# Last layer of a graph network kernel: the order of the second product's turn and copy, and how the maxima of the logits are taken

## What is computed

```python
a = (m1_s @ W_alpha).reshape(e, H, AS_)          # H = 4 heads
a = jnp.where(a > 0, a, 0.2 * a)
a = jnp.sum(a * alpha_dot, axis=-1, keepdims=True)
amax = jax.ops.segment_max(a, dst, num_segments=n)
ex = jnp.exp(a - amax[dst])
den = jax.ops.segment_sum(ex, dst, num_segments=n)
...
agg = jax.ops.segment_sum(alpha * h, dst, num_segments=n)
```

## Time and profile before

| | before |
|---|---|
| median of 3 runs | 12696.42 us (12687.43 to 12728.43) |
| the profiled execution | 12681.68 us, span 12679.8 us |
| PE busy | 8726.2 us (69%) |
| DVE busy | 7658.1 us (60%) |
| POOL busy | 7121.7 us (56%) |
| ACT busy | 4658.1 us (37%) |
| mean granted TensorE clock | 0.818 of full speed |

### The profile page before, as it was taken

The page is one execution under the profiler, slowest core; times in us unless marked ns, Lnnn a source line. Parts: engine busy times, 40 slices in busy tenths (PEclk is TensorE's granted clock), DMA queues, the critical chain, the costliest instruction groups (busy, mean ns, idle before and its releaser), DMA issues. The chain is left out here.

```text
span 12679.8 us, 243067 instructions
## 1 busy us (share of the span) xinstructions
PE 8726.2 (69%) x60118; PEld 6156.2 (49%) x60119; DVE 7658.1 (60%) x26426; ACT 4658.1 (37%) x15787; POOL 7121.7 (56%) x12018
## 2 busy tenths in 40 slices
PE   2222222278888567777757777868888888888887
PEld 1000000056666344444445555437777777777776
DVE  5333333356666443444434554878888888888887
ACT  0000000035555233333312221026666666666665
POOL 2666666645555344344336663017777777777775
PEclk8555555578888777777758888979999999999998
DMA  4000000022222211111123332930000000000000
GB/s 135 25 25 24 24 24 25 16 49 58 56 57 57 51 46 45 44 45 45 37 61 79 80 80 63 198 65 22 21 21 21 21 21 21 22 21 22 21 21 22
DMA packets 828472, 567.97 MB, mean 45 GB/s; under 512 B 588110, under 2 KB 763941, under 8 KB 825674
## 3 DMA queue, kind: packets, MB, share of 16 engines
q0 software_dynamic: 218720, 330.70, 9.8%
q1 hardware_dynamic: 596842, 196.50, 8.5%
q10 hardware_dynamic: 12480, 35.51, 0.8%
HBM read 482.70 MB, written 79.57 MB: 44 GB/s over the span
## 5 line engine op out<-in xcount | busy, mean ns | idle before, releaser
L585 PE MATMUL rank<-onehots,upper_h 128*128 128x427 f16 x812 | 407.5, 502 | 1683.9 <-remote 1014.9
L1327 POOL DMA_INDIRECT l1s_tile_rows<-node_table,l1s_tile_rows x864 | 835.3, 967 | 1260.1 <-DMA l1s_tile_rows<-rows_by_src 1018.7
L2444 POOL DMA_INDIRECT l_source_rows<-node_table,l_edge_rows x866 | 877.3, 1013 | 973.4 <-DMA l_edge_rows<-rows_by_dst 712.1
L908 POOL DMA_INDIRECT l_source_rows<-node_table,l_edge_rows x880 | 867.7, 986 | 743.4 <-DMA l_edge_rows<-rows_by_dst 393.1
L1710 POOL DMA_INDIRECT l2s_node_rows<-node_table,l2s_edge_rows x864 | 866.5, 1003 | 650.0 <-issue 243.0
L605 POOL DMA_INDIRECT rows_by_src<-row_s,pos_i x812 | 782.7, 964 | 706.7 <-issue 414.0
L585 PEld LDWEIGHTS rank<-onehots,upper_h 128*128 128x128 f16 x812 | 84.0, 103 | 2222.2 <-remote 1168.3
L605 POOL DMA_INDIRECT rows_by_dst<-row_d,pos_i x812 | 785.0, 967 | 270.6 <-issue 266.6
L1470 ACT COPY l1s_outer<-l1s_p_outer 128x1024 f32<-128x1024 f32 x304 | 307.4, 1011 | 1324.7 <-remote 885.3
L1740 PE MATMUL l2s_p_sum<-l2s_rows_by_edge,l2s_node_onehot 128*128 128x352 f32 x1728 | 695.0, 519 | 125.8 <-issue 125.3
L976 PE MATMUL l_p_sum<-l_messages,l_node_onehot 128*128 128x384 f32 x1728 | 676.0, 540 | 126.6 <-DVE l_messages L1025 81.0
(11 more groups left out here) (580 smaller groups left out, 27290.6 us busy)
## 6 DMA issues: line engine op xcount, KB each, us to landing
l_xv_by<-h_turned_l SPq DMA_DIRECT2D x120, 320.0 KB
l_source_rows<-node_table,l_edge_rows POOLq DMA_INDIRECT x1746
l_xs_by<-h_turned_l SPq DMA_DIRECT2D x40, 640.0 KB
rows_by_src<-pad_rows_s ACTq DMA_DIRECT2D x16, 1053.0 KB
l1s_tile_rows<-rows_by_src SPq DMA_DIRECT2D x216, 78.0 KB
l2s_edge_rows<-rows_by_src SPq DMA_DIRECT2D x216, 78.0 KB
l_edge_rows<-rows_by_dst SPq DMA_DIRECT2D x220, 72.0 KB
l_edge_rows<-rows_by_dst SPq DMA_DIRECT2D x433, 36.0 KB
```

The costliest lines, as they stand in the source:

```text
L908: pool.indirect_dma_start(xg[k][:, s, :], None, K["table0"], bass.IndirectOffsetOnAxis(ap=pay[k][:, s, D_SRC:D_SRC + 1].bitcast(U32), axis ...
L1327: pool.indirect_dma_start(ring[:, t, 0:XW], None, table, bass.IndirectOffsetOnAxis(ap=ring[:, t, XW + S_DST:XW + S_DST + 1].bitcast(U32), ...
L2444: pool.indirect_dma_start(xg[u][:, s, :], None, K["table0"], bass.IndirectOffsetOnAxis(ap=pay[u][:, s, D_SRC:D_SRC + 1].bitcast(U32), axis ...
```

## The change

On TensorE the six transpositions of the second product move ahead of the three front transpositions, and on ScalarE the copies of the turned second product move from behind the front copies to right behind tanh. `masked` becomes `spread_logits`: the product with `apart` is left out, and each head's product with `sel` starts its own sum. On ScalarE the bf16 copy of the one-hot is replaced by an affine copy to float32, 1e30 times (one-hot - 1), in four buffers named `apart`. On VectorE each reduction of 512 columns is replaced by `take_max`: a semaphore increment and, for each of the two heads, one fused instruction that adds the mask in SBUF to the logits in PSUM, writes the sum to SBUF and its maximum to a column of `qm`. `qm` moves from PSUM to SBUF, where L2732 reads it.

```diff
-        sel, apart = sb("sel", [P, HEADS, P], BF16), sb("apart", [P, P], BF16)
+        sel = sb("sel", [P, HEADS, P], BF16)
...
-            hot_t, hot_tb = four("onehot_turned", [P, PAIR * P]), four("onehot_turned_b", [P, PAIR * P], BF16)
-            pay_t = sbi("edge_rows_turned", [P, P])
+            hot_t, apart = four("onehot_turned", [P, PAIR * P]), four("apart", [P, PAIR * P])
+            pay_t, masked = sbi("edge_rows_turned", [P, P]), sbi("masked_logits", [P, 2, PAIR * P])
...
-            mn, drop, shrink = (sbi(n, [P, HEADS]) for n in ("new_max", "max_step", "shrink"))
+            qm, mn, drop, shrink = (sbi(n, [P, HEADS]) for n in ("pair_max", "new_max", "max_step", "shrink"))
...
-            qm = p_r[:, 0, 512 - HEADS:512]
...
-                    def masked(half, u):
-
-                        nc.tensor.matmul(p_m[:, :, :], apart[:, :], free(hot_tb[u][:, :], [0, 2], [1, PAIR * P]), start=True, stop=False, skip_group_check=True)
+                    def spread_logits(half):
+
                         for j in range(2):
-                            ins = nc.tensor.matmul(p_m[:, j, :], sel[:, 2 * half + j, :], a3_t[:, :], start=False, stop=True, skip_group_check=True)
+                            ins = nc.tensor.matmul(p_m[:, j, :], sel[:, 2 * half + j, :], a3_t[:, :], start=True, stop=True, skip_group_check=True)
...
-                            wait("a3_copied", -1)
-                            wait("rbf_scaled")
-                            wait("hot_made")
-                            front_turn(ahead_u)
-
                             for n in ("b_done", "b_scaled", "b_crossed"):
                                 wait(n, -1)
...
                                 ins.then_inc(m["g_turned"], 1)
+
+                            wait("a3_copied", -1)
+                            wait("rbf_scaled")
+                            wait("hot_made")
+                            front_turn(ahead_u)
...
-                    def front_halves(u):
-                        nc.scalar.copy(hot_tb[u][:, :], hot_t[u][:, :])
+                    def front_apart(u):
+                        nc.scalar.activation(apart[u][:, :], hot_t[u][:, :], ACT.Copy, bias=-NEVER, scale=NEVER)
...
                             nc.scalar.activation(th[:, :, :], logits[:, :, CS:D], ACT.Tanh, scale=0.5).then_inc(m["tanh_done"], 1)
+                            wait("heads_done", -1)
+                            for s in range(PAIR):
+                                wait("g_turned", 0, s + 1)
+                                nc.scalar.copy(g_t[s][:, :], p_t[:, s, 0:PT]).then_inc(m["g_copied"], 1)
                             wait("val_made", -1)
...
                             front((u + 1) % 4)
-                            wait("heads_done", -1)
-                            for s in range(PAIR):
-                                wait("g_turned", 0, s + 1)
-                                nc.scalar.copy(g_t[s][:, :], p_t[:, s, 0:PT]).then_inc(m["g_copied"], 1)
...
+                    def take_max(h, off):
+                        dve.sem_inc(m["dve_seen"], 1)
+                        for j in range(2):
+                            ins = nc.vector.tensor_tensor_reduce(masked[:, j, :], p_m[:, j, :], off[:, :], 1.0, -NEVER, ALU.add, ALU.max, qm[:, h + j:h + j + 1])
+                        ins.then_inc(m["max_taken"], 1)
...
-                            nc.vector.tensor_reduce(qm[:, 0:2], p_m[:, :, :], AX.X, ALU.max).then_inc(m["max_taken"], 1)
+                            take_max(0, apart[(u - 2) % 4])
...
-                            nc.vector.tensor_reduce(qm[:, 2:4], p_m[:, :, :], AX.X, ALU.max).then_inc(m["max_taken"], 1)
+                            take_max(2, apart[(u - 2) % 4])
...
-                            TT(mn[:, :], top_b, qm, ALU.max).then_inc(m["max_made"], 1)
+                            TT(mn[:, :], top_b, qm[:, :], ALU.max).then_inc(m["max_made"], 1)
```

11 lines of the change are left out of this document (5 added, 6 removed).

## The result

The changed kernel takes 12541.17 us (median of 6 runs, 12534.64 to 12582.6) against 12701.51 us for the kernel before, timed beside it (6 runs, 12687.43 to 12728.43). The ratio is 0.9877, 95% interval 0.9861 to 0.9892. It is faster by 1.2%, inside the range and on the forecast side, but by 160 us where 228 were forecast: the forecast's own range ended at 12540, so the time lies at its edge, towards the rival of growing blocks (12578). The profiled executions are 12681.68 and 12534.64 us, 147 us apart.

The account below looks back on a forecast made before the run. TensorE and VectorE were nearly full, TensorE waiting for ScalarE's copies; VectorE would become the bound. 3 x 0.47 + 0.70 = 2.11 us a pass, 108 passes, 228 us: 12468 us against the median; range 12335 to 12595.

Parts of the forecast that it names:

- the forecast's own range: Whole kernel: 12410 to 12540 us around 12468, VectorE the new bound with moderate blocks; chance 0.55.
- rival of growing blocks: "Blocks grow": L2732, L2734, L2736 and L2745 on VectorE each lose part of a GpSimd cross product; 12578 us, chance 0.20.
- a pair: Two fused 256-element sums on VectorE replacing one reduction: 0.68 us, 0.72 with 0.04 for the semaphore increment.
- The rival of half rate: Fused pair on VectorE runs at half rate, 0.53 us more per pair, twice a turn; 12926 us, chance 0.07.
- Nothing gained: Heads wait for the leaky step until S+6.16 as for the copies; only the pass start gains; 12690 us, chance 0.05.
- ScalarE's delays: Gate, dots' copy and front copies go about 0.5 to 0.9 us later in ScalarE's order; priced at nothing.
- the signs named: For blocks on VectorE: durations of L2732 and L2745 above their floor in many turns.
- the heads can start 0.37 after L2740 starts: TensorE's heads after VectorE's leaky step L2740: 0.27 for the step plus 0.1 for the signal.
- its 0.23 for blocks: Plain turn: 0.23 us added for VectorE operations blocked by GpSimd, between 0 - 0.15 and 0.5.
- the 1.04 taken: VectorE from L2730 to the leaky step L2740: 1.04 us in the turn shown, a small block already included.
- The pass start: Turn that starts each pass of four: heads earlier by 0.70 us, ends 0.5 and 0.8.
- the fused sums as 0.22 spent on VectorE: Each fused pair costs 0.11 us more than the reduction, 0.22 a turn, taking mask products off TensorE.

Follow-up runs that it names:

- the second increment: Changed kernel with `dve.sem_inc` written twice ahead of each pair of fused sums on VectorE; ratio 0.9885 to the kernel before.
- the leaky step last: TensorE's head products wait for the first copy, then the leaky step, tanh wait dropped: 0.9900 on the changed kernel, 0.9869 on the kernel with only the reordering.
- the copy in the gap: The last run: reordering alone, leaky step as TensorE's last wait, copy of the maxima moved between second product's dots and their sum; 10742.2 us, ratio 0.9844.
- the product put back: Changed kernel with one 512-column product, its result overwritten, ahead of each pair of head products; 12500.33 us beside 12624.41 before, single run.
- fewer waits: Kernel with only the reordering; TensorE waits for both copies at once, then the leaky step, tanh wait dropped; ratio 0.9858.
- two steps behind: Kernel with only the reordering; VectorE's sum of the dots and max step moved behind the leaky step and value sum; 12655.04 us, ratio 1.0015.
- e1: Kernel before with only the order of turns and copies changed, mask products and reductions kept; 12451.26 us beside 12624.41, ratio 0.9861.

## Why the prediction was right, and where it fell short

**Right: the mechanism.** The wait for ScalarE's copies turned into one on the leaky step; VectorE became full; L2516 is gone; the fused sums follow one another after 0.34 and a pair takes 0.69 (forecast 0.68, and 0.72 with its increment); VectorE's wait before the head spread is 0.13 (forecast under 0.2). The rival of half rate is refuted: 418 ns for 256 elements, which would have been near 685 (0.53 more a pair, half of it each). "Nothing gained" is refuted too: the heads start at S+5.89, not 6.16. ScalarE's delays cost nothing: no VectorE wait for the gate appears. "Blocks grow" is not what happened either: 0.46 for 0.36. But the blocks fell on other operations than the signs named. The new maximum is above its floor in 45% of the plain turns, the scaled leaky step in 8%; the max step and the copy of the maxima in 95% and more.

**The step that failed** is "the heads can start 0.37 after L2740 starts", with 0.1 for the signal. It measured 0.57: 0.27 for the leaky step, 0.15 for its signal, and 0.15 for the wait for the first copy, which stands behind it in TensorE's queue although its signal has long come. The plain turn, forecast with its 0.23 for blocks placed ahead of the leaky step, against the medians:

```
                 first max  L2733  leaky  heads  spread  turn
forecast         1.10       4.05   5.32   5.69   7.38    8.81
measured         1.25       4.16   5.32   5.89   7.58    9.01
```

The leaky step is where it was forecast by luck: two errors cancel, 0.11 late up to L2733 and 0.11 early from there. (a) The first maximum came 0.15 late: the head products do start 0.21 sooner, but the pair begins 0.19 after their end where the reduction began 0.04 after it; the second increment, at 0.10 each, puts most of the difference on the increment, priced at 0.04. (b) From L2733 to the leaky step it was 1.16, 0.12 more than the 1.04 taken, where 0.23 had been added. (The 1.04 of the turn shown in the earlier trace rows was a lightly blocked one; the median of the kernel before is 1.29. A piece of the chain that varies should be read over many turns.) From there on the whole miss is one term: 0.57 for 0.37. In 324 plain turns (three of each pass) this 0.20 is 65 us. The pass start, 9.51 against 10.09, gained 0.58 of its 0.70, within its ends, which in 108 passes is 13 us more. Together 78 us, where 68 are missing from the medians and 81 from the profiled executions (228 less 160, 228 less 147).

Was it that term that bound, though? Only in part. In the changed kernel VectorE's own row was 0.13 us ahead of the heads, so of the 0.20 no more than 0.13 could have come back. And in the runs not even that came: with the leaky step last the heads started 0.16 sooner, with the copy in the gap 0.19, and the turn stayed. Two chains end within 0.13 us of each other at the head spread: leaky step, signal, heads; and VectorE's own row, whose length is not fixed, because GpSimd's blocks grow when it moves forward (0.46 to 0.62) and shrink when it moves back (to 0.23 with the product put back). The prediction counted blocks once, as a sum to be added. They act as a spring: of 0.22 put in, 0.10 came out; of 0.16 taken out at the heads, nothing. That the blocks are GpSimd's is shown by the run without the cross product; that they answer a shift in this way is read from the medians of these few runs and was not tested by itself.

**The sign of the parts.** The prediction counted the fused sums as 0.22 spent on VectorE for the mask products' time on TensorE. The balance is zero before the reordering (0.9994), and after it, with VectorE full, the mean turn is 0.06 us worse, inside what the intervals leave open. TensorE's saving was real where it stood, and bought nothing behind it: the six turns of the first product start at S+1.13 in the kernel before and after alike, though a product of 0.21 had gone from ahead of them.

**A better version?** The reordering alone, with fewer waits and with the leaky step last lie at 0.9858 to 0.9869, the changed kernel at 0.9877, with overlapping intervals. The 0.9844 of the copy in the gap is of a chip with a shorter whole; its mean turn, 9.08, is that of the leaky step last. In the mean turn the reordering alone, 9.09, is ahead of 9.15. More than that can't be claimed.

Open: whether the blocks would fall with another order of GpSimd's own five operations wasn't tried; nor was a VectorE row with its holes filled without moving anything past the leaky step.

## What to carry to other kernels

When a wait is removed, write down the end of every other chain that meets at the same instruction, VectorE's own row included; shortening one chain is worth at most its lead over the next, 0.13 us here, and less where the next one grows. Price a signal with the waits that stand behind it in line: 0.15 us here when it is the last, 0.30 when one more follows. Before moving an instruction of a full engine, look at what it separates: here a result that was read by the very next instruction cost 0.18 to 0.23 us, and with two such pairs all that the reordering had gained was lost.

## What the hardware showed unexpectedly

A block ends with a GpSimd instruction, not with the cross product as a whole: the max step L2739 is held in 271 of 277 plain turns of the changed kernel and ends 0.02 us after such an instruction does. A 0.28 us operation can last up to 0.86 us (L2748, 276/279/862 ns). It lands on one VectorE instruction or another with the phase, in stable states: the same program ran its plain turns at 8.85 or 8.93 us, by which instruction was hit.

ScalarE takes up the logits at varying times, though TensorE's rows are the same: from the start of the last values products (the pair's second two) to the copy of the alphas it is 0.64 us in the kernel before, 0.89 after, 1.04 with the leaky step last, 1.00 with two steps behind and 0.64 again in the last run. No run here settles why. It cost something only where the leaky step hung on tanh.

The last run's chip took 10908.12 us for the kernel before, where the others took 12624 to 12702. The mean granted clock of the profiled execution was 0.88 there and 0.81 to 0.82 elsewhere; in the loop of the last layer it is 1.00 (2.4 GHz) on both, and the plain turn 8.94 on both. The difference lies outside the loop that the change touches (3914 and 3913 us long in e1 with the leaky step last and in the last run), so there a saving of 166 us is a larger share.
